# Two graph layers on one core: the other stages of neighbouring graphs, cut into 512-column pieces, are put between the attention tiles; the scores keep one pair of PSUM banks

## The reference, cut to what matters

```python
# x (16, 1024, 256) f32, adj (16, 1024, 1024) int32, mostly 0, else 1
h = relu(layernorm(x))
Q, K, V = h @ Wq.T + bq, h @ Wk.T + bk, h @ Wv.T + bv      # 8 heads of 32
s = einsum('bhnd,bhmd->bhnm', Q, K) * 32 ** -0.5
attn = softmax(where(adj == 0, -inf, s))                   # per head and row
x = x + einsum('bhnm,bhmd->bhnd', attn, V) @ Wo.T + bo
h = relu(layernorm(x))
e = leaky_relu(einsum('bid,bjd->bij', h * a_0, h), 0.2)    # a_1..a_3 where adj is 2..4
x = x + softmax(where(adj == 1, e, -9e15)) @ h
```

## Time and profile before

| | |
|---|---|
| time, median of 3 runs (range) | 3986.06 us (3979.12 to 3994.07) |
| span of the profiled execution | 3976.3 us, so 9.8 us less than the median time |
| PE busy | 3669.7 us, 92% |
| DVE busy | 3128.6 us, 79% |
| ACT busy | 2267.1 us, 57% |
| POOL busy | 674.9 us, 17% |
| mean granted TensorE clock | 0.967 |
| PE waits in all for `al` (L773 <- L611) | 161.1 us in 63 waits |

### The profile page before, as it was taken

How to read it: one execution, slowest core, us unless ns; L and a number is a source line. 1 busy time by engine, 2 the same in 40 slices (tenths; PEclk the granted TensorE clock), 3 DMA queues, 4 the chain that set the end, 5 groups by cost and what they waited for, 6 DMA issues and landing times.

```text
span 3976.3 us, 94630 instructions
## 1 busy us (share of the span) xinstructions
PE 3669.7 (92%) x34096; PEld 2908.9 (73%) x34096; DVE 3128.6 (79%) x5926; ACT 2267.1 (57%) x3940; POOL 674.9 (17%) x440
## 2 busy tenths in 40 slices
PE   6989989899998989989899898998989989899998
PEld 5777777777777767777777777776777767777776
DVE  6968778687886978869788696886968869688785
ACT  3837547275573845738456384663836638366482
POOL 1021030310303103031020301203012030120300
PEclk8999999999999999999999999999999999999999
DMA  5041220403204032040310503104031040311300
GB/s 151 2 105 36 60 82 2 117 25 70 71 2 118 23 76 66 2 131 10 81 61 4 137 2 83 59 15 126 2 89 53 21 121 2 95 47 31 99 2 12
DMA packets 129070, 227.67 MB, mean 57 GB/s; under 512 B 20672, under 2 KB 71104, under 8 KB 128448
## 3 DMA queue, kind: packets, MB, share of 16 engines
q1 hardware_dynamic: 128448, 219.50, 20.3%
HBM read 101.98 MB, written 16.78 MB: 30 GB/s over the span
## 4 chain that ended last, share of the span: by engine, by line
PE 68%; SPq 11%; issue 9%; DVE 7%; DMA 2%; ACT 1%; DVEq 0%; POOL 0%; POOLq 0%; ACTq 0%
PE pT L856 21%; PE ps L837 15%; PE pO L873 13%; SPq L220 11%; PE ps L773 8%; PE pO L975 7%; PE pT L908 2%; DMA adj_half<-in_adj_dram 2%; PE pT L963 2%; DVE pt L525 1%; DVE most L483 1%; DVE sm L667 1%; PE pO L884 1%; DVE sm L510 1%; DVE sm L674 1%
## 5 line engine op out<-in xcount | busy, mean ns | idle before, releaser
L349 ACT ACTIVATE sm<-sm,mn 128x1024 f32<-128x1024 f32 x1024 | 1179.5, 1152 | 454.8 <-DVE mn L510 452.5
L510 DVE CUSTOM_DVE_ANT_0 sm<-ps,bias 128x1024 f32<-128x1024 f32 x1024 | 1250.9, 1223 | 197.5 <-PE ps L837 178.0
L856 PE MATMUL pT<-ident,sm 128*128 128x128 f32 x8192 | 1098.6, 276 | 40.3 <-DVE pt L525 37.1
L856 PEld LDWEIGHTS pT<-ident,sm 128*128 128x128 f32 x8192 | 961.3, 142 | 218.5 <-DVE pt L525 52.8
L837 PE MATMUL ps<-ks,qs 96*128 96x512 f32 x2048 | 754.4, 451 | 4.6 <-issue 3.7
L525 DVE COPY pt<-pT 128x512 f32<-128x512 f32 x1024 | 702.4, 686 | 31.5 <-PE pT L856 30.8
L873 PE MATMUL pO<-pt,v 128*32 128x128 f32 x16384 | 649.7, 278 | 4.8 <-DVE pt L525 4.8
L359 ACT COPY pt<-pT 128x512 f32<-128x512 f32 x1024 | 583.2, 570 | 56.7 <-PE pT L856 56.4
L290 POOL TENSOR_SCALAR bias<-adj_half 128x512 bf16<-128x512 int32 x240 | 468.0, 1950 | 864.3 <-DMA adj_half<-in_adj_dram 855.7
L873 PEld LDWEIGHTS pO<-pt,v 128*32 128x32 f32 x16384 | 388.2, 109 | 170.1 <-issue 170.1
L975 PE MATMUL pO<-h,pt 128*128 128x256 f32 x2048 | 463.0, 379 | 0.0
(11 more groups left out here) (104 smaller groups left out, 3526.5 us busy)
## 6 DMA issues: line engine op xcount, KB each, us to landing
adj_half<-in_adj_dram SPq DMA_DIRECT2D x256, 256.0 KB, 2.8
ks<-pt SPq DMA_DIRECT2D x384, 128.0 KB, 2.4
qs<-pt SPq DMA_DIRECT2D x384, 128.0 KB, 2.4
xf<-in_x_dram SPq DMA_DIRECT2D x16, 1024.0 KB, 8.0
x<-in_x_dram SPq DMA_DIRECT2D x16, 1024.0 KB, 5.7
out_dram<-x SPq DMA_DIRECT2D x128, 128.0 KB, 2.9
x<-in_L_gnn_Wq_dram SPq DMA_DIRECT2D x1, 256.0 KB, 2.8
x<-in_L_gnn_Wk_dram SPq DMA_DIRECT2D x1, 256.0 KB, 3.1
```

The costliest lines, as they stand in the source:

```text
L349: nc.scalar.activation(sm[:, t % RING, :], sm[:, t % RING, :], ACT.Exp, scale=-1.0, bias=mn[:, t:t + 1], accum_out=den[:, t:t + 1]).then_i ...
L510: nc.vector.tensor_tensor_reduce(out=sm[:, t % RING, :], in0=ps[t % 2][:, :], in1=bias[:, node, :], scale=1.0, scalar=3e38, op0=ALU.add, o ...
L856: last = nc.tensor.transpose(pT[c][:, j * P:(j + 1) * P], sm[:, t % RING, m * P:(m + 1) * P], ident[:, :])
```

## The change

The program becomes a software pipeline over graphs. A pass of the loop is one `stage(b)`: the 64 attention tiles of graph `b`, and between them the output projection and layer 1 of graph `b - 1` and the front of graph `b + 1`. A table, `background`, says which piece stands in which of the 64 steps. Each piece fills at most one PSUM bank (512 columns). Pieces alternate between two banks of their own, `pG0` and `pG1`. To make room, the scores have one buffer of two banks, `ps`, for every tile, and the scores of `s + 2` wait until tile `s + 1` is masked. The value product of attention has one bank, `pA`, and is issued whole in every fourth step; `pB` holds the softmax factors and layer 1's value product. `pt` has four slots for attention and one for layer 1; layer 1 has one `sm` slot. The transposes of both layers share `pT`.

```diff
-SLOTS = 8
+def background(earlier, later):
+    pieces = {s: [] for s in range(TILES)}
+    for n in range(4):
+        pieces[n].append(("value", n))
+    if earlier:
+        for n in range(4):
+            pieces[n + 1].append(("out", n))
+            pieces[n + 9].append(("h", n))
+        for t in range(NT):
+            pieces[14 + 3 * t].append(("edge", 2 * t))
+            pieces[15 + 3 * t].append(("edge", 2 * t + 1))
+    if later:
+        for n in range(4):
+            pieces[48 + n // 2].append(("front", n))
+        for n, s in enumerate((50, 51, 52, 53, 59, 60, 62, 63)):
+            pieces[s].append(("qk", n))
+    return pieces
...
-        ps = [ctx.enter_context(nc.psum_tensor(f"ps{i}", [P, N], F)) for i in range(2)]
-        pO = [ctx.enter_context(nc.psum_tensor(f"pO{i}", [P, HALF], F)) for i in range(2)]
+        ps = ctx.enter_context(nc.psum_tensor("ps", [P, N], F))
+        pG = [ctx.enter_context(nc.psum_tensor(f"pG{i}", [P, HALF], F)) for i in range(2)]
+        pA = ctx.enter_context(nc.psum_tensor("pA", [P, HALF], F))
+        pB = ctx.enter_context(nc.psum_tensor("pB", [P, HALF], F))
...
-                for t in range(TILES):
-                    if t + 2 < TILES:
-                        scores(b, t + 2)
-                    transposes(t)
-                    if t >= HG:
-                        values(t // HG - 1, t % HG)
+                for s in range(TILES):
+                    if s + 2 < TILES or later:
+                        pe.wait_ge(masked, TILES * b + s + 2)
+                        if s + 2 < TILES:
+                            scores(b, s + 2)
+                        else:
+                            scores(b + 1, s + 2 - TILES)
+                    if s == 13 and earlier:
+                        general = read_flag(o)
+                    if earlier and 17 <= s < 17 + 3 * NT and s % 3 == 2:
+                        pe.wait_ge(pt_made[0], TILES * b + s)
+                        pe.wait_ge(pt_made[1], TILES * b + s)
+                        edge_transposes(o, (s - 17) // 3)
+                    for kind, n in pieces[s][0:1]:
+                        product(kind, n)
+                    if earlier and 18 <= s < 18 + 3 * NT and s % 3 == 0:
...
+                        edge_values(o, (s - 18) // 3, (0,))
+                    if earlier and 19 <= s < 19 + 3 * NT and s % 3 == 1:
+                        edge_values(o, (s - 19) // 3, (1, 2, 3))
...
+                    if s and s % HG == 0:
+                        values(b, s // HG - 1, not earlier)
...
+                    if earlier and 17 <= s < 17 + 3 * NT and s % 3 == 2:
+                        pe.wait_ge(lpt[0], NT * o + (s - 17) // 3 + 1)
+                        pe.wait_ge(lpt[1], NT * o + (s - 17) // 3 + 1)
+                    transposes(b, s, not earlier)
+                    for kind, n in pieces[s][1:2]:
+                        product(kind, n)
```

1581 lines of the change are left out of this document (892 added, 689 removed).

## The result

The changed kernel takes 4170.64 us (median of 4 runs, 4160.54 to 4184.89) against 3986.54 us of the kernel before on the same chip. The ratio is 1.0471, 95% interval 1.0443 to 1.0499: slower by 4.7%, 137 us over the forecast of 4,034 and outside its range.

The account below looks back on a forecast made before the run. PE, busy 92% of the span, was taken to bound the kernel: 218.1 us of work, 27.6 of waits and 1.3 extra give 247 per graph. With the ends, 4024 of span, so 4034 us, 1.2% slower; range 3,905 to 4,150.

Parts of the forecast that it names:

- the ring: Single score buffer: scores and mask wait on each other, no step under 2.25 us; PE stands 0.71 in 15 light steps.
- The whole value product: Attention on PE: value products issued whole take 30.2 us a graph instead of 37.1 in quarters, saving 6.9.
- The hand-offs: Single `pT` and `pt`: PE's waits for copies, 24 x 0.3 = 7.2 us a graph, plus 2.5 after edge transposes.
- The normalisation on ACT lies beside DVE's work: Front of the next graph: normalisation on ACT, busy 57%, was charged nothing.
- The last layer 1 is as long as now: End of the kernel, after the last attention: layer 1 still takes 89 us.
- The turn: Loop's jump back: PE's wait charged at 2.1 us a graph, bounds 0 and 3.3.
- 1.3 us for the slow clock: Per graph: slow-clock work behind the turn and hand-overs of DVE's added operations, 1.3 us, bounds 0 and 6.
- Stacks and second load costed at nothing: SP's stack transfers and second adjacency load stay hidden, cost 0; if not, DVE stands at `most`, 4 us a graph.
- Faster: Rival, chance 0.29: ring and hand-offs cost half, covered by pieces and PE's early issue; about 3,850 us.
- Steps lengthen: Rival, chance 0.15: late extra DVE operations in layer 1 and light steps add 8 to 12 us a graph; 4,145 to 4,200.
- Clock falls in light steps: Rival, chance 0.04: light steps run at 1.2 GHz, 15 us more a graph; 4,240 us.
- Branches: Rival, chance 0.01: skipped general paths after 16 half tiles each cost an instruction fetch, 30 us a graph; 4,450 us.

Follow-up runs that it names:

- e13: The kernel before with one score buffer for attention's tiles 3 to 63, value products kept in quarters: 4147.12 us, ratio 1.0409.
- e4: The changed kernel with the edits of e1, e2 and e3 together: 4055.21 us, ratio 1.0173 to the kernel before.
- e12: The kernel before with each attention value product issued whole, one step behind its group, instead of in quarters: 4123.44 us, ratio 1.0359.
- e14: The kernel before with one score buffer and whole value products ahead of the transposes, no neighbouring graph's pieces: 4464.86 us, ratio 1.12.
- e1: The changed kernel with POOL's `residual` moved behind the masks of nodes 3 and 4: 4127.14 us, ratio 1.0356 to the kernel before.
- e16: The changed kernel with `nmr` made by eight one-column operations with one tensor source each, `residual` in its place: 4139.79 us, ratio 1.0391 to the kernel before.
- e2: The changed kernel with the last section's stores issued three tiles later: 4124.92 us, ratio 1.0345 to the kernel before.
- e3: The changed kernel with two graphs in the loop's body, 7 passes instead of 14: 4145.29 us, ratio 1.0391 to the kernel before.
- e9: e4 with the pairs of `most` moved to steps 40, 44, 48, 52, 56, 60 and 8, ahead of DVE's copy: 4094.74 us, ratio 1.0279 to the kernel before.
- e10: e4 with `leaky` ahead of DVE's copy in the 16 edge steps: 4072.44 us, ratio 1.0228 to the kernel before.
- e5: e4 with two more unused 512-column matmuls on PE in each of seven light steps: 4063.66 us, ratio 1.0198 to the kernel before.

## Why the prediction was wrong

The direction was right and the forecast's own mechanism, the ring, is there with its size. What failed are three terms outside it: one put at nothing, one taken over from before, one too small. Its steps:

- **The ring, 2.25 us, and 0.71 in a light step.** Right: 2.24 in e13, in the same row form as the earlier trace rows, and in steps 41 and 57 of the changed kernel. PE waits for `masked` 19.5 us a graph, and 16.6 in e4 (264.8 us in 282 waits), where the forecast's terms for it (10.7, 0.5, 3.4 and 1.2) sum to 15.8.
- **The whole value product "saves 6.9" of PE's work.** The work is saved; taken alone it costs 9 us a graph of time (e12), because DVE sets the light tiles. In the sum it did no harm, since the light steps were priced by the ring. By the forecast's own terms the new attention with nothing in it costs 48 x 0.71 + 16 x 0.3 - 6.9 = 32 us more a graph; e14 measured 30.2.
- **The hand-offs, 9.7 us.** Too much: PE's two waits for copies in the rows above are 48.5 + 21.6 us, 4.4 a graph. With 26.1 us that PE stands at the attention transposes of step 38, where the code has it wait for the copies of an edge transpose, they are 6.0.
- **"The normalisation on ACT lies beside DVE's work", costed at nothing.** The step that failed in the middle. The part of it that DVE does, `nmr`, was not priced at all, and it landed beside POOL's `residual`. e1 gives 43.5 us, and e1 and e16 together show that what is held is an operation with both tensor sources in SBUF. The Trainium skill (SBUF — State Buffer, "Who interferes with whom") says that a VectorE instruction with two SBUF inputs contends with a GpSimd instruction that reads SBUF, and that the later one waits until the first is done. Here the trace agrees: `nmr` starts 0.07 us behind `residual` and takes 4.47 us in the median, where one source takes 0.2. The rule was open to me and the forecast did not use it; an estimate by it alone would have priced the step at `residual`'s length less its own, 4.52 - 0.17 = 4.3 us a graph.
- **"The last layer 1 is as long as now", 89 us.** The step that failed at the end. From the last attention mask to the end it is 144.3 us, against 95.9 before. I had not read SP's order in the last section. e2 gives 45.7 back.
- **The turn, 2.1 of 0 to 3.3.** Mis-sized, and outside its bounds: 3.6 us by the medians of e3, 4.3 by its graphs, 5.7 by those of e4. The charge took half a Q product off the stop of DVE; in fact PE stands 3.0 us itself, and the slow clock behind the stop comes on top. Over 13 turns the difference to 2.1 is 20 to 47 us.
- **1.3 us for the slow clock.** Too little. The profiled execution has 502 us at 1.2 GHz, 31 a graph, twice as much as before. The slow stretches lie at the same places: in all 14 middle graphs within steps 5 to 8 and 45 to 48, in 9 of them in steps 54 to 56, and behind 12 of the 13 turns. The value products of steps 8 and 56 take 3.09 and 3.16 us in the median instead of 1.95, 2.3 us a graph in these two alone.
- **What is left:** 4170.64 - 4034 - 43.5 - 45.7 - 20 = 27 us with the turn at 3.6, and nothing with the turn at 5.7. Which of the two holds in the changed kernel the runs do not decide, so how much the slow clock costs apart from the turn is argued, not shown.
- **Stacks and second load costed at nothing.** Right in the changed kernel, where DVE never waits for an adjacency load in the stages, so the rival of the unhidden transfers falls. But it is right by little: e9 uncovers 62 us by moving one pair of `most` two steps.
- **The rivals.** *Faster* fell: in e14 and in steps 41 and 57 the ring stands in full. *Steps lengthen* gave the measured time, 4,145 to 4,200, by the wrong reason, so that is luck: e10 shows that DVE's queue is not what sets the edge steps. *Clock falls in light steps* was half right. The clock falls at their end and behind them, and not to 1.2 GHz throughout, so the rule of the Trainium skill that spoke for it (TensorE: Matmul & The Clock Gate, "A second HAM failure mode: psum-queue depth-cycling") has some support in the stretch at 0.72; filling the stops moved the slow stretches and did not remove them (e5). *Branches* fell in size: outside the turn and step 38 PE waits for issue at the edge transposes in 36 cases, 13.2 us in all, under 1 us a graph and not 30.

With the three repairs and 7 turns fewer the forecast's sum would be 4034 - 7 x 2.1 = 4,019; e4 measured 4,055. The six turns that stay are 9 to 22 of the remaining 36 us. The rest lies at the ends more than in the middle: a middle graph of e4 without a turn is 245.5 us, and the forecast's 247 less its 2.1 is 244.9. The first full stage starts at 259 us instead of 58 + 190 = 248, and the last layer 1 is 7 us longer than before, while the last stage is some 6 shorter than the 229 forecast. Its verdict on the idea itself, slower, stands, but not at 1.2%: with the first two repairs and as many turns as before the sum of the medians is 4170.64 - 43.5 - 45.7 = 4,081 us, 2.4% slower.

## What to carry to other kernels

Before stages are spread into a loop that is paced tile by tile, measure what the room for them costs: put the smaller buffers and the coarser products into the old kernel alone. Here that structure cost 30 us a graph and the spreading won 28. The loop's turn is worth a look first: seven graphs in the old loop's body won 1.0% alone. Idle time of an in-order engine covers only work that is queued ahead of its wait; what stands behind it delays the next hand-over in full. And when order changes, look again at every small instruction with two SBUF sources beside a long GpSimd one, and at each section that is written out on its own, the last one above all.
